# Products of two loaded heads on TensorE around the first taps, the first taps operand in two loads, and B's parts behind the first x parts

## The reference

```python
x_m = x * mask
K = 2 * einsum('hn,hnl->hl', Cs, exp(P)).real
x = x + mask * (irfft(rfft(x_m, 1024) * rfft(K, 1024))[..., :512] + x_m * D[:, None])
gate = x @ W_gate.T + SCALE * (x @ A_gate[i].T) @ B_gate[i].T
up   = x @ W_up.T   + SCALE * (x @ A_up[i].T)   @ B_up[i].T
act  = silu(gate) * up
x = x + act @ W_down.T + SCALE * (act @ A_down[i].T) @ B_down[i].T
```

## Time and profile before

| what | us |
|---|---|
| median of 3 runs (lowest to highest) | 531.21 (531.13 to 532.42) |
| the profiled execution's own time | 531.22 |
| its span, first to last instruction | 529.4 |
| TensorE busy | 495.7 (94%) |
| VectorE busy | 289.9 (55%) |
| ScalarE busy | 197.7 (37%) |
| GpSimd busy | 51.3 (10%) |
| share of the 16 DMA engines used by the one queue | 59.8% |

### The profile page before, as it was taken

One profiled execution on the slowest core, in us unless ns is written; L12 is line 12 of the kernel. 1 busy time (PEld: TensorE's weight loads), 2 busy tenths in 40 slices (PEclk: granted clock), 3 DMA queues, 4 the chain that ended last, 5 costly groups with the idle time before them and its releaser, 6 DMA issues.

```text
span 529.4 us, 9990 instructions
## 1 busy us (share of the span) xinstructions
PE 495.7 (94%) x2940; PEld 450.2 (85%) x2940; DVE 289.9 (55%) x613; ACT 197.7 (37%) x411; POOL 51.3 (10%) x59
## 2 busy tenths in 40 slices
PE   0099969999999999999999999999999999999997
PEld 0099957989898989999999999898989898989996
DVE  7884336746464545546464646373736474645541
ACT  6780037533343333333343433342434243434330
POOL 1007622000000001010100101010100010101000
PEclk9999999999999999999999999999999999999999
DMA  7799995547565656565655556465647465655520
GB/s 285 274 322 360 361 350 126 141 98 166 112 159 112 153 122 156 111 146 121 135 121 142 125 139 131 109 155 111 157 87 175 97 164 112 156 116 149 108 64 21
DMA packets 175443, 82.74 MB, mean 156 GB/s; under 512 B 128034, under 2 KB 157282, under 8 KB 175426
## 3 DMA queue, kind: packets, MB, share of 16 engines
q1 hardware_dynamic: 175426, 82.54, 59.8%
HBM read 63.46 MB, written 19.04 MB: 156 GB/s over the span
## 4 chain that ended last, share of the span: by engine, by line
PE 86%; DVE 5%; DMA 4%; SPq 2%; issue 1%; ACT 0%; POOL 0%; DVEq 0%; POOLq 0%; ACTq 0%
PE ps_u L1105 21%; PE ps_g L1105 21%; PE ps_db L1066 13%; PE ps_da L1066 13%; PE ps_g L1032 4%; PE ps_u L1032 3%; PE ps_x L1058 2%; PE ps_g L1115 2%; PE ps_g L1116 2%; PE ps_u L1115 2%; PE ps_u L1116 2%; DMA xrow<-x_sq 1%; SPq L315 1%; PE ps_da L1172 1%; DMA b_raw<-btab 1%
## 5 line engine op out<-in xcount | busy, mean ns | idle before, releaser
L523 ACT CAST b_spl<-b_raw 64x512 fp32r<-64x512 f32 (+1 forms) x96 | 51.7, 570 | 68.4 <-PE ps_u L1116 34.6
L1105 PE MATMUL ps_g<-w_hi,x_hi 128*128 128x512 f32 (+1 forms) x192 | 73.0, 380 | 4.3 <-DVE x_lo L989 4.3
L1105 PE MATMUL ps_g<-w_hi,x_lo 128*128 128x512 f32 (+1 forms) x192 | 71.9, 374 | 0.0
L1105 PE MATMUL ps_g<-w_lo,x_hi 128*128 128x512 f32 (+1 forms) x192 | 71.8, 374 | 0.0
L1105 PE MATMUL ps_u<-w_hi,x_lo 128*128 128x512 f32 (+1 forms) x192 | 71.5, 372 | 0.0
L1105 PE MATMUL ps_u<-w_hi,x_hi 128*128 128x512 f32 (+1 forms) x192 | 71.4, 372 | 0.0
L1105 PE MATMUL ps_u<-w_lo,x_hi 128*128 128x512 f32 (+1 forms) x192 | 71.3, 371 | 0.0
L870 DVE TENSOR_TENSOR b_spl<-b_raw,b_spl 64x512 fp32r<-64x512 f32 (+1 forms) x96 | 57.9, 629 | 19.3 <-ACT b_spl L523 17.8
L927 DVE TENSOR_TENSOR h_act<-h_act,ps_u 128x512 f32<-128x512 f32 (+1 forms) x48 | 30.4, 633 | 56.7 <-PE ps_u L1116 37.1
L1066 PE MATMUL ps_da<-wd_hi,ht_hi 128*128 128x288 f32 (+1 forms) x176 | 52.1, 296 | 0.0
L1066 PE MATMUL ps_db<-wd_lo,ht_hi 128*128 128x288 f32 (+1 forms) x176 | 51.9, 295 | 0.0
(11 more groups left out here) (169 smaller groups left out, 892.0 us busy)
## 6 DMA issues: line engine op xcount, KB each, us to landing
a_raw<-atab SPq DMA_DIRECT2D x64, 152.0 KB, 2.3
toep<-kpad SPq DMA_DIRECT2D x16, 512.0 KB, 5.7
b_raw<-btab SPq DMA_DIRECT2D x128, 64.0 KB, 2.2
h_raw<-hrow SPq DMA_DIRECT2D x30, 256.0 KB, 3.0
um<-xr SPq DMA_DIRECT2D x16, 256.0 KB, 4.2
x<-xT SPq DMA_DIRECT2D x8, 512.0 KB, 5.9
w_raw<-wgu SPq DMA_DIRECT2D x8, 512.0 KB, 8.9
xrow<-x_sq SPq DMA_DIRECT2D x64, 64.0 KB, 2.2
```

The lines of the kernel that those rows point to most:

```text
L523: nc.scalar.copy(b_spl[b_rows(slot), up, 0:w], b_raw[b_rows(slot), up * w:(up + 1) * w]).then_inc(b_hi, 1)
L1105: T.matmul(ps[:, 0:w], xs[:, kb, :], ws[:, kb, col:col + w], start=(kb == 0 and xs is x_hi and ws is w_hi), stop=False)
```

## The change

On TensorE, ten products of two heads of x that are loaded already stand ahead of `taps(0)` and eight behind it (64 weight columns, 256 moved columns, F32). Their result is not used; `conv(0)` overwrites the PSUM buffer. They wait for both loads of the first group of x. `toep` of pair 0 is loaded with one DMA per head, and the two halves of `conv(0)` wait for one each. The parts of B for chunk 0 go behind the two casts of x on ScalarE and behind `square_x(0)` on VectorE. Piece 14 gets its low part on GpSimd; the casts of pieces 15 and 16 move one place forward on ScalarE, and the low parts of pieces 15 and 16 on VectorE likewise.

```diff
+        WD_POOL = NP_GU + 2
...
-                sp.dma_start(toep[:, slot, :, :], shifted_taps(pair)).then_inc(toep_in[slot], 16)
+                if pair == 0:
+                    for h in range(2):
+                        sp.dma_start(toep[:, slot, h, :], shifted_taps(pair)[:, h, :]).then_inc(
+                            toep_half if h == 0 else toep_in[slot], 16)
+                else:
+                    sp.dma_start(toep[:, slot, :, :], shifted_taps(pair)).then_inc(toep_in[slot], 16)
...
             for n in range(2 * KB, NP_POOL):
                 rem_part(n)
+            rem_part(WD_POOL)
...
-            act.wait_ge(k_ready, NG)
-            b_hi_part(0, 0, 0, 0)
-            b_hi_part(0, 0, 0, 1)
...
                     top_part(NP_GU + 2)
+                    top_part(NP_GU + 3)
                     turned_hi_part(0)
...
-                    top_part(NP_GU + 3)
+                    top_part(NP_GU + 4)
...
                 silu(2)
                 if first:
-                    top_part(NP_GU + 4)
                     top_part(NP_GU + 5)
...
             nc.scalar.copy(x_hi[:, :, (NH - 4) * BT:P], xt[:, :, (NH - 4) * BT:P]).then_inc(xhi_ok, 1)
+            act.wait_ge(k_ready, NG)
+            b_hi_part(0, 0, 0, 0)
+            b_hi_part(0, 0, 0, 1)
...
-                    rem_part(NP_GU + 2)
+                    rem_part(NP_GU + 3)
...
-                    rem_part(NP_GU + 3)
+                    rem_part(NP_GU + 4)
...
-                        rem_part(NP_GU + 4)
                         rem_part(NP_GU + 5)
...
-            b_lo_part(0, 0, 0, 0)
-            b_lo_part(0, 0, 0, 1)
...
             square_x(0)
+            b_lo_part(0, 0, 0, 0)
+            b_lo_part(0, 0, 0, 1)
...
-                pe.wait_ge(toep_in[slot], 16 * (pair // RC) + 16)
+                pe.wait_ge(toep_half if pair == 0 else toep_in[slot], 16 * (pair // RC) + 16)
...
+                    if pair == 0 and h == 1:
+                        pe.wait_ge(toep_in[0], 16)
...
+            def idle_product(n):
+
+                for _ in range(n):
+                    T.matmul(ps_g[0][0:NB, 0:KB * NB], x[:, 0, 0, :], x[:, 1, :, :].rearrange("p k b -> p (k b)"),
+                             start=True, stop=True)
+
+            pe.wait_ge(x_in[0], 32)
+            idle_product(10)
             taps(0)
+            idle_product(8)
             conv(0)
...
-                pe.wait_ge(w_rem_dve, len(pieces) - NP_POOL)
+                pe.wait_ge(w_rem_dve, len(pieces) - NP_POOL - 1)
+                pe.wait_ge(w_rem_pool, NP_POOL + 1)
```

More of the change, by code:

```diff
@@ L166, in program @@
         toep_in = [sem(f"toep_in{i}") for i in range(RC)]
+        toep_half = sem("toep_half")
         um_in = [sem(f"um_in{i}") for i in range(RC)]
```

## The result

The changed kernel takes **533.04 us** (median of 20 runs, 530.13 to 536.76), the one before 531.25 (20 runs beside it, 530.13 to 532.42): ratio **1.0032**, 95% interval 1.0018 to 1.0047. It is slower by 0.3%, and the forecast was 529.1, between 527.3 and 531.6. The quickest run of both kernels is the same, 530.13; the changed one's reach further up, over 6.6 us where the other's cover 2.3. The profiled execution took 533.13, near the median, with a span of 531.2 against 529.4.

The account below looks back on a forecast made before the run. The prediction took the time from 107.70 as fixed and asked which chain, mostly loads, reaches tile 1's first `lora` last. Gains of 1.26 at pair 8 and 0.8 at the seam, 2.06, gave 529.1 us, range 527.3 to 531.6.

Parts of the forecast that it names:

- Eight more products ... end near 23.4: Kernel head: the eight products behind `taps(0)` take 3.9 us and end before the first half of `toep` can land.
- Cost of the ten nothing: Kernel head: the ten products start at 10.5, take some 7 us and end by 18, before `taps(0)` at 18.85.
- the rival by which it would not: Kernel head: the products don't raise the clock and pair 0 starts later, still cold; 531.8 to 533.3 us, chance 0.13.
- So pair 0 starts 1.6 us earlier and warm: Kernel head: pair 0 starts near 24.7 in place of 26.27, at full clock, taking about 2.4 us.
- 23.8 to 25.9: Kernel head: when the first half of pair 0's `toep` lands, issued at 21.7; 24.7 was taken.
- Gain at pair 8: 0.36 + 0.90 = 1.26: Stage one: pair 8 starts 1.26 us earlier, 0.36 from an earlier copy and 0.90 from filling unused DMA share.
- TensorE keeps its pace: From pair 8 on: loads need 321 GB/s, under 396, so the end of the stage comes 1.26 us earlier.
- TensorE is 4.6 ahead here: Seam after stage one: `base` of tile 0 starts 2.9 us earlier and 1.7 us of lower clock is avoided.
- It gives most of it back: Seam to tile 1's first `lora`: later waits take back the 4.6 us lead until 0.8 us is left.
- B of chunk 1: Tile 0: it lands at 85.33, its `lora` runs at 86.7, TensorE idles 2.4 us and 2.25 are left.
- A at `lora_a(1)`: Tile 1: A lands at 98.1, GpSimd is done at 99.5, and waiting for it takes some 1.2 us more.
- The sum: Whole kernel: 1.26 us from stage one plus 0.8 us from the seam, 2.06 us faster in all.

Follow-up runs that it names:

- e17: The changed kernel without the ten products ahead of `taps(0)`, all else kept: ratio 1.0002 to the kernel before.
- e6: The kernel before with B's parts behind the first x parts and GpSimd's pieces 8 to 11 held until `t_lo` is written: ratio 1.0022.
- e5: The kernel before with only B's parts of tile 0 moved behind the first x parts: ratio 1.0005.
- e14: The kernel before with only the piece moves (piece 14 to GpSimd, the next two one place forward): ratio 1.0024, median 532.43 us.
- e13: The changed kernel with piece 14 back on VectorE and the next two pieces in their old places: ratio 1.0008 to the kernel before.

## Why the prediction was wrong

- **"Eight more products ... end near 23.4"**: right, 23.29. Cost of the ten nothing, `taps(0)` at 0.68: right. The clock did rise while narrow products ran, to 1.00 from 15.63, so the rival by which it would not is out, and that 533.0 lies in its range of 531.8 to 533.3 is chance. (The Trainium skill's rule on transposes, TensorE: Matmul & The Clock Gate, PE-mode transpose, does not reach to narrow plain products, by these rows.)
- **"So pair 0 starts 1.6 us earlier and warm"**: wrong on both. The first half landed at 25.8, at the upper end of 23.8 to 25.9: it took 4.0 where the whole took 4.2. So half the bytes saved 0.2, and the rest of the 0.4 is an earlier issue; the loads issued right behind it share the same DMA engines. I took no account of the idle time that this leaves, 2.54, though I had the pattern in the earlier trace rows: 4.30 idle, then 0.50. I took 1.4 of idle time as harmless, which it was; 2.54 and 2.06 I did not price at all.
- **"Gain at pair 8: 0.36 + 0.90 = 1.26"**: this is the step that failed. Pair 8 started at 53.01, 0.44 later, not at 51.3. I read unused share as room to be filled. From 41 to 46 it was (314 to 375 GB/s); from 36 to 41 the rate fell from 298 to 258, and all of that from 36 to 38 (344 to 243), as nothing could be asked for between 33.7 and the landing of group 1's store at 36.28. That store, 2.4 in my sum, took 3.90, so pair 4 started at 40.76 and not at 40.0. What filled the queue after it stood ahead of group 2's small store, 6.41 where it was 5.2. Then the clock fell, and "TensorE keeps its pace" fell with it: of the 2.12 by which the last pair ended later, 0.44 are the landing and 1.68 the clock.
- **"TensorE is 4.6 ahead here"**: right as to the seam (1.38 idle, no 0.50). **"It gives most of it back"**: right as to the sum, from the last pair to the arrival 35.08 against 35.67, 0.59 kept where I had 0.8. That it came near is luck, as I was wrong as to the takers: not B of chunk 1 (no wait) nor A at `lora_a(1)` (no wait), but `t_lo` under GpSimd, 2.49, and 1.91 in tile 1. I had put piece 14 on GpSimd beside VectorE's work at no cost.
- **The sum.** -1.26 became +2.12 and -0.8 became -0.59: +1.53 at the arrival. No rival of mine had a slower kernel with the clock rising as intended. The deeper fault is where I took the limits one by one, from pair 4 to pair 8 to B to A. Behind them stands a queue that all four share, and an order of issue behind `load_y`; my views of TensorE's waits do not show it, and the chain of work that ended last does, in its rows from 79 on. The last cause of the 1.53 stays open: without the ten products the loss is gone (e17, 1.0002), but which of the late queue, the stretch on VectorE and the waits in stage one carries it is not shown.

## What to carry to other kernels

Before pricing waits of the busiest engine one at a time, follow the chain that ended last over the whole head: if its long pieces are DMAs and an issuing queue, a faster engine moves only its own waits. Then ask how far behind the next chain is: here TensorE's own was 0.6 us shorter, so neither a faster TensorE nor an earlier queue could give more than that alone. Filler work that is made faster by other filler work ends sooner: the ten products here opened the very gap that the eight were to close. A queue that gets large loads sooner delays the small stores behind them, on which the next loads depend. And where runs spread over several us, a trace has to be held against the median of its kernel before it explains anything.

## What was not expected of the hardware

- A VectorE subtraction that starts while a GpSimd one runs makes little way until that one has ended. The piece at 90.74 took 2.59: GpSimd's ended at 92.25, and 1.08 more were needed of a work of 1.23. The first two `t_lo` ended at 82.36 and 84.03, 0.15 behind pieces of GpSimd. All eight `t_lo` instructions of tiles 0 and 1 in the changed kernel (durations in ns, least, median, greatest):

```profile
L922 DVE TENSOR_TENSOR t_lo<-t_m,t_hi x8: 284/288/1648, 81.1 to 108.8; 64x128 fp32r<-64x128 f32 x8
```

  0.29 us of work took up to 1.65. It goes both ways: GpSimd's four pieces took 6.66 in the kernel before and 9.12 in e6. `t_m`, which has one operand in PSUM (`ps_x`), took its 0.29 beside such a piece as well (at 81.84 in the kernel before).
- While ten products that use 64 of 128 weight columns ran, from 10.56 on, the granted clock rose to 1.00 (from 15.63 on). It then fell behind some idle times and not behind others of the same length: behind 2.54 and 2.06, not behind 2.49 in the same execution; behind 2.47 in e5, not behind 2.46 in e17 or 3.44 in e14; in e13 behind 1.59 and not behind 2.40. So a fall can't be read off the length of one wait.
- A store of 16 KB took 2.4 us or 3.90 behind few loads, and 6.41 in a full queue.
